# Two transformer layers on one core: another order of the opening, and sums finished ahead of row maxima in the odd rounds

## The reference

```python
x = x + xattn0(layernorm(x), ctx)      # 16 heads of 16, biases, clipped probabilities
x = x + ffn0(layernorm(x))             # inputs and weights quantised to 4 bits by blocks of 16; silu(gate)*up, width 704
x = x + xattn1(layernorm(x), ctx, mask)  # 16 heads of 64, masked keys
x = x + ffn1(layernorm(x))             # fixed point, piecewise linear gelu, width 1024
```

```python
scores = q @ k.T / 4
attn = softmax(scores - max(scores))
attn = clip(attn, 1e-12, None)
attn = attn / sum(attn)
ctx = attn @ v
```

## Time and profile before

| what | before |
|---|---|
| median of 3 runs | 927.75 us (927.74 to 927.95) |
| the profiled execution, its own time | 927.82 us |
| its span in the profile | 926.0 us |
| TensorE busy, matmuls | 900.5 us (97%) |
| VectorE busy | 669.8 us (72%) |
| ScalarE busy | 602.1 us (65%) |
| GpSimd busy | 204.6 us (22%) |

### The profile page before, as it was taken

One profiled execution on the slowest core, in us unless ns is written; L12 is line 12 of the kernel. 1 busy time (PEld: TensorE's weight loads), 2 busy tenths in 40 slices (PEclk: granted clock), 3 DMA queues, 4 the chain that ended last, 5 costly groups with the idle time before them and its releaser, 6 DMA issues.

```text
span 926.0 us, 16209 instructions
## 1 busy us (share of the span) xinstructions
PE 900.5 (97%) x5610; PEld 601.8 (65%) x5610; DVE 669.8 (72%) x2179; ACT 602.1 (65%) x1671; POOL 204.6 (22%) x316
## 2 busy tenths in 40 slices
PE   6899999999999999999999999999999999999998
PEld 3555576767665567576675566667757655757786
DVE  5999883763989786475598978367478988837568
ACT  3888425972789643795378953499257984269845
POOL 3211001862000000486000000077400000028600
PEclk9999999999999999999999999999999999999999
DMA  9500000000000000000000010000000000000000
GB/s 294 212 1 2 29 1 23 2 1 1 1 1 25 1 28 24 1 1 2 1 0 8 18 29 1 24 1 1 1 0 1 19 7 1 1 0 2 2 1 23
DMA packets 14560, 18.35 MB, mean 20 GB/s; under 512 B 3088, under 2 KB 11664, under 8 KB 14480
## 3 DMA queue, kind: packets, MB, share of 16 engines
q1 hardware_dynamic: 12288, 15.40, 5.0%
q10 hardware_dynamic: 2064, 1.91, 0.7%
q0 software_dynamic: 128, 0.01, 0.0%
HBM read 15.21 MB, written 2.10 MB: 19 GB/s over the span
## 4 chain that ended last, share of the span: by engine, by line
PE 76%; DVE 13%; ACT 8%; issue 3%; DMA 1%; SPq 0%; DVEq 0%; ACTq 0%
PE bank L1243 28%; PE bank L1258 10%; PE bank L1526 6%; PE bank L1624 6%; PE bank L1506 6%; PE bank L1358 5%; PE bank L1414 4%; ACT ring L671 4%; DVE row_max L1050 3%; PE bank L1391 3%; PE bank L1481 1%; PE bank L1492 1%; PE bank L1251 1%; PE bank L1430 1%; ACT ring L715 1%
## 5 line engine op out<-in xcount | busy, mean ns | idle before, releaser
L463 POOL TENSOR_TENSOR rstd<-var_eps,minus_half 128x2 f32<-128x2 f32 x32 | 23.3, 734 | 533.1 <-DVE var_eps L886 533.1
L481 POOL TENSOR_TENSOR ring<-ring,row_inv 128x256 f32<-128x256 f32 x192 | 112.1, 613 | 95.4 <-DVE row_inv L1145 95.4
L556 ACT ACTIVATE ring<-bank 128x512 f32<-128x512 f32 x224 | 123.6, 612 | 14.1 <-PE bank L1258 12.6
L1258 PE MATMUL bank<-ident_s,ring 128*128 128x128 f32 x768 | 105.0, 279 | 5.1 <-DVE ring L1058 2.7
L1258 PEld LDWEIGHTS bank<-ident_s,ring 128*128 128x128 f32 x768 | 82.8, 141 | 39.2 <-issue 15.7
L715 ACT ACTIVATE ring<-ring,row_max 128x256 f32<-128x256 f32 x192 | 95.1, 497 | 17.3 <-DVE row_max L1138 17.3
L671 ACT ACTIVATE ring<-bank,row_max 128x256 f32<-128x256 f32 x192 | 88.4, 496 | 5.7 <-DVE row_max L1050 5.7
L1138 DVE CUSTOM_DVE_ANT_0 ring<-bank,maskbias 128x256 f32<-128x256 f32 x192 | 70.7, 420 | 23.4 <-issue 23.4
L1050 DVE TENSOR_REDUCE row_max<-bank 128x2 f32<-128x512 f32 x128 | 79.4, 684 | 5.9 <-PE bank L1391 5.2
L1243 PE MATMUL bank<-wgu_s,act_s 128*128 128x352 f32 x256 | 78.4, 459 | 0.0
L1243 PE MATMUL bank<-ctxT_s,wk_s 128*128 128x512 f32 x160 | 76.4, 600 | 0.0
(11 more groups left out here) (192 smaller groups left out, 1753.3 us busy)
## 6 DMA issues: line engine op xcount, KB each, us to landing
x_s<-x SPq DMA_DIRECT2D x4, 512.0 KB, 3.9
ctxT_s<-ctxT SPq DMA_DIRECT2D x4, 512.0 KB, 4.2
w_s<-w SPq DMA_DIRECT2D x2, 1024.0 KB, 16.3
out<-act_s SPq DMA_DIRECT2D x16, 128.0 KB, 1.7
wk_s<-wk SPq DMA_DIRECT2D x1, 1024.0 KB, 13.4
wv_s<-wv SPq DMA_DIRECT2D x1, 1024.0 KB, 14.7
wq_s<-wq SPq DMA_DIRECT2D x1, 1024.0 KB, 16.2
wo_s<-wo SPq DMA_DIRECT2D x1, 1024.0 KB, 17.5
```

The lines of the kernel that those rows point to most:

```text
L481: ins = pool.tensor_tensor(probs1[i % PRING1][:, a, :], probs1[i % PRING1][:, a, :], row_inv[:, i, a:a + 1].to_broadcast([P, SEQ]), ALU.mult)
L556: act.activation(probsT[u % TRING][:, :, :].rearrange("p a q -> p (a q)"), psum(at, key)[:], ACT.Copy).then_inc(drain(at, key), 1)
L1258: ins = pe.transpose(psum(at, key)[:, c * SEQ + a * P:c * SEQ + (a + 1) * P], tile[:, a, c * P:(c + 1) * P], ident_s[:])
```

## The change

It does two things.

In the opening, TensorE transposes the inputs ahead of the first key chunk, does the queries and the first scores, and only then the second key chunk. ScalarE evacuates the inputs first, then the first key chunk, and then does the step on weight piece 0; the second key chunk's evacuation moves between the exponentials of units 1 and 2. VectorE scales weight piece 1 after the maxima of round 0 instead of ahead of them. The banks move: queries to 5 and 6, the second key chunk to 7.

In the odd rounds from the third on, of all four passes, ScalarE does `inverse_sum` ahead of the first pair of transposes and VectorE does `over_sums` ahead of the round's row maxima.

```diff
--- before.py
+++ after.py
@@ -98,7 +98,7 @@
 
     jobs = Jobs()
     for c in range(KEY_CHUNKS):
-        jobs.add(("k0", c), c)
+        jobs.add(("k0", c), c if with_last_layer else 7 * c)
     if with_last_layer:
         for t in range(TILES):
             jobs.add(("v0", t), 4 + t)
@@ -107,7 +107,7 @@
     if with_last_layer:
         jobs_last_hidden(jobs)
     for c in range(KEY_CHUNKS):
-        jobs.add(("q0", c), c if with_last_layer else 7 * c)
+        jobs.add(("q0", c), c if with_last_layer else 5 + c)
     if with_last_layer:
         jobs_last_out(jobs)
     else:
@@ -685,20 +685,22 @@
                         key_first = r > 1
                         if key_first:
                             layer1_key(at, r - 1)
+                        if r >= 3 and r % 2 == 1:
+                            inverse_sum((r - 3) // 2)
                         for i in (first, first + 1):
                             evacuate_probsT(at, 0, i)
                         if not key_first:
                             layer1_key(at, r - 1)
                         if with_weights and r >= WEIGHTS_FROM:
                             evacuate_weights(at, r - WEIGHTS_FROM)
-                        if r >= 3 and r % 2 == 1:
-                            inverse_sum((r - 3) // 2)
                         for i in (first + 2, first + 3):
                             evacuate_probsT(at, 0, i)
                         if with_weights and r >= 2 and r % 2 == 0:
                             piece_steps(r // 2 + 1)
                     if r < ROUNDS0:
                         for i in round_units0(r):
+                            if i == 2 and with_weights:
+                                layer0_keys(at, [1])
                             exponentials(i)
                 evacuate_values(middles[units // UNITS], *VALUES_FIRST[0])
                 inverse_sum(WEIGHTED0 - 1)
@@ -800,11 +802,10 @@
             pack(wk0_s, wk0_padded, wk0_loaded, wk0_packed)
             pack(wq0_s, wq0_padded, queries_loaded, wq0_packed)
             act.wait_ge(keys_loaded, 16 * 4)
+            layer0_inputs(opening_pass)
+            layer0_keys(opening_pass, [0])
 
             piece_steps(0)
-            layer0_keys(opening_pass, [0])
-            layer0_inputs(opening_pass)
-            layer0_keys(opening_pass, [1])
             act.wait_ge(query_mask, 6)
             for c in range(KEY_CHUNKS):
                 layer0_query(opening_pass, c)
@@ -1060,12 +1061,13 @@
                     ins.then_inc(clipped0, 1)
 
                 for r in range(ROUNDS0):
+                    if r >= 3 and r % 2 == 1:
+                        over_sums(at, (r - 3) // 2, units // UNITS)
                     for i in round_units0(r):
                         row_maxima(i)
-                    if r >= 3 and r % 2 == 1:
-                        over_sums(at, (r - 3) // 2, units // UNITS)
                     if r == 0:
                         if g is None:
+                            scale_piece(1)
                             dve.wait_ge(values_loaded, 16 * 2)
                             layer0_values(at, range(TILES))
                     for i in round_units0(r):
@@ -1215,7 +1217,6 @@
             scale_piece(0)
             query_masks()
             round_piece(0)
-            scale_piece(1)
             dve.wait_ge(consts_set, 6)
             layer0_heads(opening_pass, 0, None)
             dve.wait_ge(rest_loaded, 16 * 5)
@@ -1629,18 +1630,18 @@
             zeros = v0[:].rearrange("p t i n d -> p (t i n d)")
             for n in range(WARM_UP):
                 pe.matmul(bank[7][:], zeros[:, 0:P], zeros[:, 0:512], start=True, stop=True)
-            pe.wait_ge(wk0_packed, 1)
-            pe.wait_ge(ctx_loaded, 16)
-            layer0_keys(opening_pass, [0])
             pe.wait_ge(ident_loaded, 16)
             for h in range(HALVES):
                 pe.wait_ge(xn_ready, 2 * h + 2)
                 transpose_xn(opening_pass, 0, h, xn0)
-            layer0_keys(opening_pass, [1])
+            pe.wait_ge(wk0_packed, 1)
+            pe.wait_ge(ctx_loaded, 16)
+            layer0_keys(opening_pass, [0])
             pe.wait_ge(wq0_packed, 1)
             layer0_queries(opening_pass)
+            layer0_scores(opening_pass, 0)
+            layer0_keys(opening_pass, [1])
             pe.wait_ge(values_loaded, 16 * 2)
-            layer0_scores(opening_pass, 0)
             for t in range(TILES):
                 layer0_values(opening_pass, t)
             layer0_heads(opening_pass, 0, True)
```

## The result

The changed kernel takes **929.38 us** (median of 19 runs, 927.92 to 930.06); the kernel before, run between them, 927.79 (19 runs, 927.38 to 928.12). The ratio is 1.0014, interval 1.0008 to 1.002: slower by about a seventh of a per cent, which is less than the 0.2% set as the bound of "no change". The forecast was 925.5 with a range to 927.5, so it is missed by 3.9 us.

A forecast was written before the change was run, and what follows sets the result against it. TensorE matmul time was taken as the bound, with VectorE setting the pace in the opening pass's rounds. From 927.82, -0.2 + 0.8 (opening) - 1.9 (opening-pass rounds) - 1.0 (crossings) = -2.3 gave 925.5 us, range 923.7 to 927.5.

The forecast's parts named there:

- Opening, order of TensorE and ScalarE: Opening: scores start at 18.41 instead of 21.27; ScalarE's weights step and the rounding behind it come 0.41 late.
- A meeting that is new: Opening: moved scaling's line 840 on VectorE runs beside GpSimd's bias addition, losing 0.8 us, ends 0 and 0.85.
- Rival 1: Opening: GpSimd and VectorE do not disturb one another at 23.7; time 924.7; chance 0.23.
- Rounds of the opening pass: Opening pass: TensorE's wait for line 1042 goes and VectorE's idle time shrinks, gaining 1.9 us, ends 0 and 2.35.
- Rounds of the crossings: Three crossings: 0.25 regained per place less a new 0.14 wait leaves 0.11 each, 1.0 us gained in all.
- 9 places (3 in each of 3 crossings): Crossings: count of places where 0.25 us each goes, 2.25 in all before the new wait is set against it.
- TensorE waits 0.14: Crossings: new wait at the second transposes, since line 678 now stands ahead of two evacuations they need.
- Rival 4: Odd rounds: line 678 moved ahead delays TensorE's transposes by 0.56, deciding from 0.25 per round; 931.0; chance 0.05.
- Rival 2: Opening: TensorE's clock falls in a 2.2 to 3.0 us gap after the values, costing 1.9; 927.4; chance 0.08.

The follow-up runs named there:

- the three products alone: Changed kernel plus three unneeded 512-column matmuls on TensorE in the opening, behind VectorE's first evacuation of the values: 927.06 us.
- all mended: Changed kernel with GpSimd's bias addition later, three unneeded matmuls in the opening and two ahead of the second output product: 926.13 us.
- the sums part with its wait filled: Old opening with the sums moved ahead, plus two unneeded products in TensorE's wait ahead of the second output product: 926.08 us.
- sums part: Only the sums ahead of the maxima, with their evacuation moved ahead, on the old opening of the kernel before: 926.5 us.
- the run with the bias moved: Changed kernel with GpSimd's first addition of the bias to x moved behind its product on weights piece 1: 928.2 us.
- the repeat: The changed kernel run and profiled again with no edit: 929.36 us.
- the opening alone: Changed kernel with both halves of the sums part taken back, leaving only the opening's new order: 929.86 us.
- filled wait: Changed kernel with two unneeded products (four matmul instructions) in TensorE's wait ahead of the second output product: 927.95 us.
- the two kernels with all edits: Changed kernel with bias later and both waits filled, 926.13 us; the same with line 678 between the two evacuations, 926.37 us.

## Why the prediction was wrong, by its own steps

**The account.** At a mean clock of 0.999 or 1.0 the three products alone ran at 926.9 to 927.25, all mended at about 926.1, and the sums part with its wait filled at 926.1. So the changed kernel's 929.4 is 927.8, less 1.7 for the sums part, plus about 0.85 for the collision, plus about 2.4 for TensorE's clock. Without the last term it would be 927.0, inside the range. Two steps failed: the clock, put at nothing in the sum and at 0.08 as a rival, cost 2.4; the crossings, put at 1.0, gave 0.3. The split between collision and clock is rough, since a collision lengthens the wait behind which the clock falls: by the run with the bias moved the collision alone is 0.1 to 0.5. What the opening's order is worth by itself stays open: the run with all mended shows no gain from it, but there the filling held up the transposes by 0.95 us.

**Opening, order of TensorE and ScalarE: right.** In the repeat, where the warm-up was short, the scores start at 18.03 (18.41 predicted), the step on the weights at 15.29 (15.33) and the maxima at 19.27 (19.62). Not foreseen was that the warm-up itself varies: its eight matmuls took 5.19 to 6.72 us over the profiled runs. With a long one VectorE waits for line 664; with a short one, or a late transfer, it meets GpSimd. The first normalisation comes at 26.98 and 27.11 in these two profiles, and between 26.59 and 27.88 in all with the new order and the bias in its place, not at 26.25.

**A meeting that is new: right that it costs, in the wrong place, with too narrow ends.** I took line 840 (841 now) as the one exposed and 0.85, the end of the addition, as the most. The small multiply ahead of it was hit instead (1.56 in the repeat, 1.34 with the opening alone), or, with a late load, line 841 by 1.97. I placed GpSimd's 2.35 us by one trace, whose start hangs on a transfer that came between 21.0 and 22.8.

Both rows that I weighed were misread. The 1.43 for a pair is one instruction held:

```profile
42.86 1.18 DVE L1058 TENSOR_SCALAR ring<-ring,row_inv 128x256 f32<-128x256 f32 x1
```

It ends at 44.04, 0.15 after the mask's conversion (41.12 + 2.77 = 43.89); the second of the pair kept its length. And line 840 "kept its 0.96" beside GpSimd's small step because it had started first. GpSimd was held instead: the step that takes 0.84 there, ending 0.09 after line 840, takes 0.24 where nothing is beside it:

```profile
21.24 0.24 POOL L492 TENSOR_SCALAR b_s<-b_s 128x8 f32<-128x8 f32 x1 [11.53 <-DMA wo_s<-wo]
21.47 2.35 POOL L488 TENSOR_TENSOR x_s<-x_s,bo_s 128x1024 f32<-128x1024 f32 x1
```

So before the change the rows already showed that the one that starts first goes on and the other stands until about its end. Rival 1 had no row for it. The Trainium skill (GPSIMD Engine Reference, section Specifications) names contention for instructions in a two-port mode and for those with two SBUF inputs. The traces agree for the second kind, 0.96 to 2.93; the 0.19 to 1.75 is of an instruction with one SBUF input, which would have to be of the first kind, and no row shows its mode.

**Rounds of the opening pass: right, a little large.** 39.44 became 38.00, so 1.44 for 1.9.

**Rounds of the crossings: miscounted and mis-sized.** The price of a stall was right: from the key chunk behind the transposes to the product it was 2.08 and is 1.82, 0.26 less. But the wait that replaces it, put at 0.14, is 0.21: 0.19 ahead of the transposes and 0.02 within them. A round gained 0.05, not 0.11. And there are six such places, not nine. TensorE waited for the sums in rounds 3 and 5 of each crossing, not in round 7; the other three of the nine waits of the earlier trace rows are those of the opening pass, the 1.0 among them. The products of rounds 5 and 7 in the first crossing, before:

```profile
295.09 1.07 PE L1414 MATMUL bank<-ring,v 128*32 128x256 f32 x16 [0.20 <-DVE big_c L1042]
308.72 1.07 PE L1414 MATMUL bank<-ring,v 128*32 128x256 f32 x16
```

Six times 0.05 is 0.3, and that is what is seen: with the sums part and the filled wait, the first output sum of the opening pass is 1.44 sooner (86.25), the last of the last crossing 1.73 (767.24 for 768.97). The step that failed is "9 places (3 in each of 3 crossings)", together with "TensorE waits 0.14", a difference of ends taken from rows to a tenth of a microsecond. Since the order of the three instructions on ScalarE makes no difference, it is most likely the end of the last of them, the second evacuation, that holds the round. Rival 4's mechanism is this one, at 0.2 a round, short of the 0.25 from which it decides.

**TensorE's clock: the step that cost the sign.** Rival 2 had place and mechanism right, with a wait of 2.2 to 3.0 us reckoned there and 1.9 to 3.4 found. Its chance of 0.08 rested on clocks of 1.00 read behind a wait of 1.24 us; that a short wait is harmless in one profile says nothing of one twice as long. And it named one place only. The second output product is another: its wait grew from 1.7 to 2.4 because TensorE comes to it 1.62 us sooner (92.03 for 93.65), VectorE's product over the sums only 0.92 (93.99 for 94.91). So part of the gain turned into idle time, and the idle time, in some executions, into a lower clock. A fall costs 0.9 to 1.5 us by most groups of runs (sums part 926.4 and 927.7; filled wait 926.69, 927.9 and 929.2), not 1.9. The 1.9 was taken from the warm-up's length, and in its rows the granted clock reads 1.00 (the number behind TensorE's busy time), before:

```profile
8.00:10.00 2.00, 2.00 (x3) 1.00 1.05 227
```

The same eight instructions took 5.19 to 6.72 us over the profiles; what lengthens them stays open.

Of the changed kernel's 19 runs 4 are at 0.998 and 928.1, 15 at 0.995 or 0.996 and 929.4; none is free of it, while the kernel before was mostly at 1.0. The Trainium skill (TensorE: Matmul & The Clock Gate, section HAM oscillation) warns that TensorE's clock falls back in waits between bursts of matmuls, and the traces agree: 1.00 went to 0.50.

Over the fourteen profiles a wait of 1.24 us ahead of the first transposes never had a fall in it or behind it (four profiles), one of 1.4 ahead of the transposes of round 2 in three of fourteen, one of 1.9 in the opening in one of two, one of 2.4 at the second output product in three of six, and in the opening all four waits between 2.1 and 3.4. The places are not independent: with only the opening's wait filled, 7 of 11 runs have a mean clock of 0.999 or 1.0, though the wait of 2.4 us still stands. Where the low time lies in the runs that were not profiled stays open, and also why the same wait is followed by a fall in one run and not in the next.

## What to carry to other kernels

When a change makes TensorE reach a wait sooner, write down how long that wait becomes, not only what was gained ahead of it. Waits that grew from 1.2 or 1.7 us to 2 or 3 cost more here than the change brought. Five unneeded products in such waits, with the collision moved away, brought it back (926.13, for 926.08 with the sums part and its filled wait). When work moves on VectorE, check it against every GpSimd instruction of some length whose start hangs on a transfer, over the whole span in which the transfer may come, and look at the lengths of both engines' instructions: the one that started second shows the hold. Count the places of a gain in the trace, each by its own row, before multiplying. And give the parts of a change their own runs: here one part beat both kernels (926.5, and 926.08 with its wait filled).

## What the hardware showed unexpectedly

A VectorE instruction over 48 columns can last until GpSimd's beside it ends: 0.19 us became 1.75, 1.53, 0.81 and 0.69 in four profiles, ending each time within 0.06 us of GpSimd's end. It works the other way too: GpSimd's step of 0.24 us over 8 columns took 0.84 and 0.60 in the two profiles in which VectorE's line 840 had started first, ending within 0.1 us of it. The reciprocal between the two exposed steps kept its 0.45 though GpSimd had started at 23.02, in its middle, and the reduction over 768 columns (line 835) its 0.94 beside GpSimd's addition. The mean granted clock of a run sorts the times of one kernel, mostly by 0.9 to 1.5 us for each 0.002. In the two kernels with all edits one run each lies 2.4 higher for one such step. In the kernel before the step is smaller, 927.7 to 928.2, and where its clock fell no profile shows: the one there is reads 1.00 up to 924 us.
